# Feed-forward moved behind the attention, attention's lead loop and start reordered

## The reference

```python
y = gelu(x @ W.T + fc_bias + low_rank(x, side) + cond)
dots = q @ k.T * SCALE; pos_attn = q @ rel_emb[clip(i - j, -64, 64) + 64] * SCALE
x = x + softmax(dots + pos_attn) @ v @ Wo + bo
z = sigmoid(xz_t + h @ U_z + vz); r = sigmoid(xr_t + h @ U_r + vr)
hh = tanh(xh_t + r * h @ U + vh); h = (1 - z) * h + z * hh       # 256 steps, each needs the one before
sel = argmax(h @ gate_w.T); rw = sigmoid(max(h @ gate_w.T))
x = x + (u * silu(g)) @ w_down[sel], g = (rw * h) @ w_gate[sel].T, u = (rw * h) @ w_up[sel].T
```

## Time and profile before

| | before |
|---|---|
| runs, us | 614.16, 595.54, 595.69; median 595.69 |
| profiled execution, us | 597.63 |
| its span, first to last instruction, us | 595.5 |
| mean granted TensorE clock | 0.993 |
| TensorE busy | 571.2 us (96%) |
| VectorE busy | 403.6 us (68%) |
| ScalarE busy | 334.0 us (56%) |
| first and last write of hist | 84.2 and 585.3 us |

### The profile page before, as it was taken

How to read it: one execution, slowest core, us unless ns; L and a number is a source line. 1 busy time by engine, 2 the same in 40 slices (tenths; PEclk the granted TensorE clock), 3 DMA queues, 4 the chain that set the end, 5 groups by cost and what they waited for, 6 DMA issues and landing times.

```text
span 595.5 us, 16935 instructions
## 1 busy us (share of the span) xinstructions
PE 571.2 (96%) x5108; PEld 503.5 (85%) x5108; DVE 403.6 (68%) x2663; ACT 334.0 (56%) x1481; POOL 14.0 (2%) x41
## 2 busy tenths in 40 slices
PE   6999999999999999999999999999999999999996
PEld 5888778999989998899989998899889888776674
DVE  2447767777777777776777677777777777556654
ACT  2544436666666666666666666666666555323332
POOL 1140000000000000000000000000000000000000
PEclk9989999999999999999999999999999999999998
DMA  6155540222222212122212222222222210000000
GB/s 199 41 177 153 167 148 3 76 77 76 77 76 77 77 60 88 61 68 75 67 53 75 76 81 77 76 77 81 77 65 64 67 41 2 1 6 2 2 2 11
DMA packets 44194, 41.38 MB, mean 69 GB/s; under 512 B 5692, under 2 KB 43848, under 8 KB 43976
## 3 DMA queue, kind: packets, MB, share of 16 engines
q1 hardware_dynamic: 43520, 38.65, 21.8%
q10 hardware_dynamic: 584, 1.64, 0.8%
HBM read 20.95 MB, written 19.33 MB: 68 GB/s over the span
## 4 chain that ended last, share of the span: by engine, by line
PE 73%; DVE 11%; ACT 8%; issue 7%; DMA 1%; DVEq 0%; ACTq 0%
PE bank L359 66%; ACT p_sb L733 6%; PE bank L464 5%; DVE rinv L859 2%; ACT hh L806 1%; DVE pt_sb L867 1%; DVE g L998 1%; DVE sg L957 1%; DVE gm L943 1%; DMA x_nat<-in_x 1%; DVE sg L950 1%; PE bank L375 1%; PE bank L589 1%; DVE q L985 1%; DVE p_sb L861 0%
## 5 line engine op out<-in xcount | busy, mean ns | idle before, releaser
L359 PEld LDWEIGHTS bank<-q,uc 128*128 128x128 f32 x512 | 76.7, 189 | 28.0 <-DVE q L985 26.6
L806 ACT ACTIVATE hh<-bank 128x4 f32<-128x4 f32 x256 | 44.3, 173 | 95.2 <-PE bank L359 92.1
L359 PE MATMUL bank<-g,u 128*128 128x4 f32 x512 | 94.5, 255 | 3.1 <-DVE g L998 0.2
L359 PEld LDWEIGHTS bank<-b,uw 128*128 128x128 bf16 x1280 | 71.8, 97 | 28.6
L359 PE MATMUL bank<-hist,u 128*128 128x4 f32 x510 | 91.9, 251 | 0.3
L359 PE MATMUL bank<-q,uc 128*128 128x4 f32 x512 | 85.6, 238 | 6.6 <-DVE q L985 3.0
L359 PE MATMUL bank<-pt_sb,y_nat 128*128 128x128 f32 x512 | 88.9, 296 | 2.7 <-DVE pt_sb L867 2.3
L796 ACT ACTIVATE trz<-bank 128x4 f32<-128x4 f32 x256 | 44.3, 173 | 80.2 <-PE bank L359 78.2
L359 PE MATMUL bank<-yT,qp 128*128 128x256 f32 x256 | 85.4, 415 | 0.0
L359 PEld LDWEIGHTS bank<-g,u 128*128 128x128 f32 x512 | 76.8, 190 | 8.0 <-DVE g L998 7.8
L359 PEld LDWEIGHTS bank<-hist,u 128*128 128x128 f32 x510 | 77.4, 192 | 0.9 <-DVE hist L1002 0.2
(11 more groups left out here) (148 smaller groups left out, 956.8 us busy)
## 6 DMA issues: line engine op xcount, KB each, us to landing
skew<-e_sb SPq DMA_DIRECT2D x32, 574.0 KB, 3.4
pos<-skew SPq DMA_DIRECT2D x128, 128.0 KB, 2.6
wkv_sb<-in_L_attn_Wkv ACTq DMA_DIRECT2D x1, 1024.0 KB, 8.1
x_nat<-in_x SPq DMA_DIRECT2D x1, 512.0 KB, 4.8
wq_sb<-in_L_attn_Wq ACTq DMA_DIRECT2D x1, 512.0 KB, 6.0
wo_sb<-in_L_attn_Wo SPq DMA_DIRECT2D x1, 512.0 KB, 3.6
out<-y_out SPq DMA_DIRECT2D x8, 64.0 KB, 2.2
ffn_nat<-in_L_ffn_w_gate SPq DMA_DIRECT2D x1, 256.0 KB
```

The lines of the kernel that those rows point to most:

```text
L359: return pe.matmul(o, w_, x_, start=start, stop=stop, skip_group_check=True)
L806: act.activation(st["hh"][:, now, :], pre(2, c, k), ACT.Tanh).then_inc(hh_ok, 1)
```

## The change

- Feed-forward: tile 0 runs in steps 186 to 217, tiles 1 to 6 begin at steps 217, 222, ... 242 and take 16 steps each, so up to three overlap; tile 7 follows the loop as before. Tiles use banks 6/7, 2/3 and 4/5 in turn, and small tiles three buffers. In tiles 1 to 6 VectorE's half-tile products are whole-tile ones (512 columns). From step 217 on, the first piece of a step stands beside, further ones between. The copy of the result moves from VectorE to ScalarE.
- Fillers: as many as bring a step to two pieces between and two beside (one beside from step 217).
- Lead loop: move_pt(n - 1) behind sums(n), where move_pt(n - 2) stood ahead of it. SyncE writes quad q + 1 ahead of the reads of quad q, for q = 1 to 5.
- Start of step 0: the two zero products for banks 0 and 1 stand ahead of the last lead unit; the seeds are ScalarE's; two of three gate inputs stand behind the product of g in step 0.
- Head: even and odd heads' products alternate, jobs and banks are reordered, the first preps come earlier; the far columns of chunks 0 and 1 are left out, nothing reads them; TensorE multiplies zeros nine times before x arrives, and VectorE writes those zeros.

```diff
+JOBS = (("q", 0, 0), ("q", 1, 1), ("rel", 0, 2), ("k", 0, 3), ("k", 1, 0), ("A", 0, 1), ("A", 1, 2), ("R", 0, 7), ("R", 1, 6),
+        ("A", 2, 3), ("A", 3, 0), ("R", 2, 5), ("R", 3, 2), ("R", 4, 7), ("R", 5, 6),
+        ("v", 0, 3), ("v", 1, 0), ("y", 0, 5), ("y", 1, 2), ("B", 0, 7), ("B", 1, 6), ("B", 2, 3), ("B", 3, 0))
+SLOW_AT, FAST_AT, FAST_STEP = 186, 217, 5
+FAST_PE = {0: (0, 1), 1: (2, 3), 2: (4, 5), 3: (6, 7), 4: (8,), 10: (19,), 11: (21,), 12: (23, 24), 13: (25, 27), 14: (28,)}
+FAST_DVE = {1: (2,), 2: (4, 6), 3: (8,), 4: (11,), 6: (15,), 10: (17,)}
+FAST_ACT = {2: (6,), 4: (10,), 5: (14,), 11: (22,), 12: (26,), 15: (30,)}
+LAST_DVE = {1: (2,), 2: (4, 6), 3: (8,), 4: (10, 12), 6: (14, 16), 10: (18, 20)}
+FAST_LEN = 16
+AHEAD = 6
+F_BANKS = ((6, 7), (2, 3), (4, 5))
+GM_WHOLE, AH_WHOLE = range(1, TILES - 1), range(1, TILES - 1)
...
+        def tiles_at(t, of):
+            if SLOW_AT <= t < SLOW_AT + CT and not (of is FAST_DVE and t - SLOW_AT in (11, 15, 17)):
+                yield 0, t - SLOW_AT
+            for tau in range(1, TILES):
+                step = t - (T if tau == TILES - 1 else FAST_AT + FAST_STEP * (tau - 1))
+                for k in of.get(step, ()):
+                    yield tau, k
+
+        def upto(tau, half, whole):
+            before = sum(1 if i in whole else 2 for i in range(tau))
+            return before + (1 if tau in whole else half + 1)
+
+        def f_bank(tau, j):
+            return bank[F_BANKS[tau % 3][j]]
...
-                skew_quad(q)
+                if q < 2 or q > AHEAD:
+                    skew_quad(q)
+                if 1 <= q < AHEAD:
+                    skew_quad(q + 1)
                 for b in range(4):
                     unskew_unit(4 * q + b)
-                if q == 4:
+                if q == AHEAD:
...
+            def both_halves(j):
+                kind, a, _ = JOBS[j]
+                free(j)
+                free(j + 1)
+                heads = job_heads(kind, a)
+                for i, even in enumerate(heads):
+                    for e in range(2):
+                        h, o, half = even + e, bank[JOBS[j + e][2]], slice(e * DH, e * DH + DH)
                         if kind == "A":
                             ins = mm(o[:, i * D:(i + 1) * D], wqT[half, h // 2, :], wkT[half, h // 2, :])
                         elif kind == "R":
                             ins = mm(o[:, i * RELS:(i + 1) * RELS], wqT[half, h // 2, :], relT[half, :])
                         else:
                             ins = mm(o[:, i * D:(i + 1) * D], wvT[half, h // 2, :], wo_sb[half, h // 2, :])
-                ins.then_inc(job_pe, 1)
-
+                        if i == len(heads) - 1:
+                            ins.then_inc(job_pe, 1)
+
+            pe.wait_ge(zeros_ok, 1)
+            for k in range(9):
+                mm(bank[4][:, :], zeros[:, 0:128], zeros[:, :])
...
+                if n == LEAD - 1:
+                    pe.wait_ge(u_ok, 4)
+                    pe.wait_ge(pt_ok, LEAD - 2)
+                    pe.wait_ge(e_dve, PREP_LEAD // 4)
+                    pe.wait_ge(q_dve, PREP_LEAD // 4)
+                    for k in range(2):
+                        ins = mm(bank[k][:, :], uw[:, 0, :], zeros[:, :])
+                    ins.then_inc(bits_set, 1)
...
+            def filler(t=0):
+                tau, free = (t - FAST_AT) // FAST_STEP, bank[4]
+                if tau >= TILES - 1:
+                    pe.wait_ge(aT_ok, 2 * (TILES - 3))
+                    free = f_bank(TILES - 1, 0)
+                elif tau >= 1:
+                    pe.wait_ge(gm_ok, upto(tau, 1, GM_WHOLE))
+                    free = f_bank(tau, 0)
+                mm(free[:, 0:FILLER], uw[:, 0, :], zeros[:, 0:FILLER])
...
-            for gate in range(3):
-                gate_input(0, gate)
+            gate_input(0, 0)
...
             def between(t):
-                s = (t - 1) // 2
+                s, there = (t - 1) // 2, 0
                 if t % 2 == 1 and LEAD + s < UNITS:
                     scores(LEAD + s)
-                elif t % 2 == 1:
-                    filler()
-                elif t and PREP_LEAD + s < UNITS:
+                    there += 2
+                elif t and t % 2 == 0 and PREP_LEAD + s < UNITS:
                     prep(PREP_LEAD + s)
-                elif t:
-                    if s == UNITS - PREP_LEAD:
-                        pe.wait_ge(e_act, by_act(UNITS // 2 - 1))
-                        pe.wait_ge(q_act, by_act(UNITS // 2 - 1))
-                    filler()
-                    if LEAD + s - 2 < UNITS:
-                        filler()
+                    there += 2
+                if t % 2 == 0 and s == UNITS - PREP_LEAD:
+                    pe.wait_ge(e_act, by_act(UNITS // 2 - 1))
+                    pe.wait_ge(q_act, by_act(UNITS // 2 - 1))
+                if t > FAST_AT:
+                    for tau, k in list(tiles_at(t - 1, FAST_PE))[1:]:
+                        tile_stage(tau, k)
+                        there += 1
+                if t:
+                    for _ in range(2 - there):
...
+                s, there = t // 2, 0
+                if t % 2 == 0 and LEAD + s - 2 < UNITS:
+                    values(LEAD + s - 2)
+                    there += 2
+                if t % 2 == 1:
                     if LEAD + s - 1 < UNITS:
                         transposes(LEAD + s - 1)
+                        there += 1
                     if s == 0:
                         project(PROJ_LAG - 1)
                     if PROJ_LAG + s < UNITS:
                         project(PROJ_LAG + s)
-                    else:
-                        spare += 1
+                        there += 1
                 if t < CT:
                     weights(t)
-                else:
-                    tile_stage(t // CT - 1, k)
-                if PROJ_LAG + s >= UNITS - 4:
-                    for _ in range(spare):
-                        filler()
+                late = t >= FAST_AT
+                for tau, k in list(tiles_at(t, FAST_PE))[:1 if late else None]:
+                    tile_stage(tau, k)
+                    there += 1
+                for _ in range((1 if late else 2) - there):
+                    filler(t)
...
+                if t == 0:
+                    gate_input(c, 1)
+                if k == 0:
...
+            act.wait_ge(vb_ok, 1)
+            act.wait_ge(bits_set, 1)
+            for gate in range(3):
+                ins = seed(cp, 0, gate)
+            ins.then_inc(seed_ok, 1)
...
-                if n >= 2:
-                    move_pt(n - 2)
                 sums(n)
+                if n >= 1:
+                    move_pt(n - 1)
                 if n < PREP_LEAD - HEADS and n % 4 == 3:
                     move_eq((HEADS + n) // 2)
...
-            move_pt(LEAD - 2)
...
+                if k in (10, 11, 12):
+                    part = slice(0, 8) if k == 11 else slice(2 * k - 20, 2 * k - 16)
+                    n = part.stop - part.start
```

More of the change, by code:

```diff
@@ L323, in _ @@
                 pool.memset(iota[:, e:e + 1], float(e))
-            pool.memset(zeros[:, :], 0.0).then_inc(zeros_ok, 1)
             pool.wait_ge(setup_act, 6)
@@ L422, in _ @@
             pe.wait_ge(job_dve, 2)
-            for j in range(5, 19):
-                job(j)
-            pe.wait_ge(job_act, 8)
-            pe.wait_ge(job_dve, 7)
             def prep(m):
@@ L482, in project @@
                 mm(bank[5][:, 0:128], vo[:, h, :], z2[:, q % Z_RING, m % 4, :], start=(h == 0), stop=(h == HEADS - 1)).then_inc(pj_done, 1)
-            for m in range(4):
+            both_halves(5)
+            pe.wait_ge(setup_act, 4)
+            both_halves(7)
+            pe.wait_ge(job_act, 5)
+            pe.wait_ge(job_dve, 4)
+            for m in range(4):
+                prep(m)
+            both_halves(9)
+            both_halves(11)
+            both_halves(13)
+            job(15)
+            job(16)
+            for m in range(4, 6):
+                prep(m)
+            job(17)
+            job(18)
+            pe.wait_ge(job_act, 8)
+            pe.wait_ge(job_dve, 7)
+            for m in range(6, 8):
                 prep(m)
@@ L668, in _ @@
                 mm(pre(2, c, k), uc[:, :], st["q8"][:, now, :], start=False).then_inc(c_pre, 1)
-            for k in range(CT):
-                tile_stage(TILES - 1, k)
+            for tau, k in list(tiles_at(T - 1, FAST_PE))[1:]:
+                tile_stage(tau, k)
+            for t in range(T, T + FAST_LEN):
+                for tau, k in tiles_at(t, FAST_PE):
+                    tile_stage(tau, k)
         @block.scalar
@@ L698, in _ @@
                                bias=ybias[:, b:b + 1]).then_inc(setup_act, 1)
-            for j in range(4, 20, 2):
-                job(j)
             def move_e(duo):
@@ L818, in job @@
                 job_move(cp, kind, a, bank[at_bank]).then_inc(job_dve, 1)
+            dve.memset(zeros[:, :], 0.0).then_inc(zeros_ok, 1)
```

(2 more changed lines are left out.)

236 lines of the change are left out of this document (115 added, 121 removed).

## The result

| | before | after |
|---|---|---|
| runs, us (same chip) | 614.16, 595.54, 595.69, 625.02 | 618.01, 617.52, 618.38, 614.84 |
| median, us | 604.92 | 617.76 |
| profiled execution, us | 597.63 | 618.01 |
| its span, us | 595.5 | 616.2 |
| mean granted TensorE clock | 0.993 | 0.900 |

The change makes the kernel slower: the ratio is 1.036, 95% interval 1.033 to 1.039. The prediction was 566.8 us, within 559 to 577. One thing must be known to read the numbers: not every run of one kernel keeps the clock (of all 31 runs of the kernel before, ten took 612 to 630 us), and ratios leave such runs out. The changed kernel had lost it in all four.

A forecast was written before the change was run, and what follows sets the result against it. Bound: each step's serial loop through VectorE, TensorE and ScalarE, 1.78 us, plus some 0.2 of feed-forward above attention's 1.81. Terms -24.4 - 4.4 - 0.6 - 2.0 - 2.5 + 5.0 = -28.9 gave 566.8 us, range 559 to 577.

The forecast's parts named there:

- the term of the last 39 steps: Last 39 steps: overlapping feed-forward tiles lengthen steps through third pieces and whole-tile operations; +5.0 us on 70.3, bounds +1 and +12.
- Rival D: Attention's steps: with less work in each, the clock falls, 1.2 us more per step, kernel slower; 2%.
- Steps 32 to 185: Attention steps of the loop, freed of feed-forward: plain steps fall to 1.813 us; -24.4 us, bounds -18 and -26.
- Rival B: Attention's steps do not fall to 1.81 but stay at 1.90, 12 us come back, 579 us; 7%.
- The lead loop: 22 attention units ahead of step 0: pt copy behind the sums shortens gaps to 1.56 to 1.76; -4.4 us.
- From the last exp to step 0: Between lead loop and step 0: seeds on ScalarE, two gate inputs moved later; -0.6 us, bounds 0 and -1.5.
- The head: Start of the kernel: two terms, order of the jobs -2.0 us and products on zeros -2.5 us.
- The alternation: Head: neighbouring 64-row products on different row halves partly overlap; -2.0 us, bounds 0 and -3.5.
- The zeros: Head: nine products on zeros before x lands bring the full clock earlier; -2.5 us, bounds 0 and -4.
- SyncE: Lead loop: the quad written ahead covers the faster loop; a gap on pos would show SyncE too slow.
- A: Last 39 steps much dearer: three overlapping tiles hold the loop, 2.2 per step, 85.8 instead of 75.2, 577 us; 13%.
- both together: Dearer late steps and attention's steps not falling to 1.81 at once, about 590 us; 5%.

The follow-up runs named there:

- experiment 2: Changed kernel, counting only stages with TensorE work as pieces, and two things beside instead of one in the late steps; median 572.71 us, ratio 0.963.
- experiment 11: Changed kernel with two things beside from step 217 on, its piece count left as it is; median 573.55 us, ratio 0.963.
- experiment 3: Kernel before, with its fillers left out in steps 216 to 218 alone; median 632.16 us, ratio 1.063.
- Experiment 5: Kernel of experiment 2 with VectorE's e and q copies in two units and ScalarE's z copy ahead of its e copy; 570.15 us, one run.
- Experiment 6: Kernel of experiment 2 with VectorE's copy of pt ahead of the sums, as in the kernel before; 575.11 us, one run.
- experiment 9: Kernel of experiment 3 with 16 fillers in a row added in step 226; 607.89 and 610.64 us.
- experiment 8: Kernel of experiment 2 with all even heads' products, then all odd ones, instead of alternating; 573.95 us, one run.
- experiment 7: Kernel of experiment 2 with SyncE's order as before, no quad written ahead; 571.13 us, one run.
- experiment 4: Kernel of experiment 1 without the nine products on zeros ahead of x; 607.12 us, one run.
- experiment 10: Kernel of experiment 2 without the nine products on zeros ahead of x; median 572.64 us of four runs.
- experiment 12: Kernel of experiment 2 with the split copies of experiment 5, up to two pieces beside, fillers ahead of them; median 567.20 us, ratio 0.952.
- experiment 1: Changed kernel, counting only stages with TensorE work as pieces, still one thing beside in late steps; median 599.68 us of ten runs.

## Why the prediction was wrong, and where it was right

**The step that failed** is the term of the last 39 steps, "+5.0". Its durations were those of rows at the full clock, and its bounds, +1 and +12, held no case in which the clock changes. Rival D had the mechanism, but "in attention's steps", at 2%, with the seven plain steps at 1.00 as its counter-evidence. There the clock indeed held. The late steps of the change were not asked the same question, although the text on the order ahead of the prediction says of them: "Two fillers beside became one piece of the oldest tile, and one filler between became three pieces." The prediction costed fillers by their time alone, 0.03 per step, as if they had no other office. They are what holds the clock: 94 of them gave 70.3 us for these steps, 28 gave 119.8, 29 gave 101.7, 65 gave 75.5. Experiments 2 and 11 show this by the edit that undoes it, experiment 3 in the kernel before without the change. D's price per step was about right in form: 1.2 us more per step was put, and the 37 steps at half clock cost (119.8 - 75.5) / 37 = 1.2.

The trace of before held a sign of it, which neither the rows nor the prediction use. These windows of the kernel before (columns as above) lie on both sides of a fall at 37.64 us, ahead of the first exp:

```profile
34.20:37.60 3.40, 3.40 (x31) 3.40 (x30) 0.74 (x3) 1.33 (x4) 2.17 (x5) 1.00 0.81 248
37.60:41.00 3.40, 3.40 (x12) 2.91 (x12) 1.86 (x11) 1.94 (x5) 3.00 (x6) 0.51 0.15 43
```

TensorE was busy for all of the 3.40 us before, 22 of its 31 products having 16 or 4 columns, and the clock halved all the same. So a fall under a busy TensorE could be seen before the change ran, not only in the sparse tail that the prediction names.

**The same term with the clock held** was right: 75.5 in experiment 2 against 75.3 worked out. Its parts too: a full cycle of five steps took 1.82, 1.82, 2.05, 2.05 and 2.11, so that three pieces cost 0.23 (0.25 was put) and a whole-tile operation 0.3 in the step whose transposes wait for it. The prediction's 0.33 for these operations was spread over three of five steps, with q late in each; it came in one.

**Steps 32 to 185:** -24.4 was put, -23.5 came (285.1 us against 284.2). By kind the plain steps took 242.1 (241.1 was put), the closing ones 32.8 (32.8) and the opening ones 10.2 (10.3), so the working was right and not only its sum. Rival B is dead.

**The lead loop** was mis-sized: -4.4 was put, -0.9 came (39.45 against 40.38). Plain gaps are 1.57, as put; gaps with a prep and a projection are 1.57 as well, not the 1.76 that the prediction took for TensorE. What was missed are the copies. VectorE's e and q copies in four units were put at 0.3 each; they cost 0.8 to 1.1, and the units ahead of three of them 0.5 more (gaps of 2.05 to 2.09), which fits ScalarE's two prep copies ahead of the z copy there. Experiment 5 moves VectorE's and ScalarE's copies together and gets 36.4, near the 36.0 that the prediction had; the share of each was not measured apart. The last gap is another 0.76 above the plain ones: 2.33, where the kernel before had 1.90. There the two zero products for banks 0 and 1 wait for a copy of pt and stand ahead of the last unit's scores. The prediction had this wait, at about 0.4, but counted it behind the last exp. Experiment 6 shows that the pt copy was the link in the plain gaps. In the first 20 gaps the change gained 1.4 (38.48 to 37.12), and the last gave 0.4 back.

**From the last exp to step 0:** 5.0 became 4.05, -1.0 where -0.6 was put, in its bounds. With the 0.4 of the zero products, which fell into the lead loop, it is -0.5, near the -0.6 that was put.

**The head** gained 3.5 until the first exp (38.82 to 35.31) where 4.5 was put, but for another reason. In the profile before, the clock rose only at 17.2 us; in the same head of experiments 3 and 9 it rose at 8.7 and 8.9, and the first exp stood at 35.35 in experiment 3. So 3.5 us of the difference to the earlier trace rows is the luck of one execution before: the changed kernel gained nothing against that head (35.31), and 1.3 us where its clock held (34.02, experiment 2). The alternation is worth 2.2 (experiment 8) as put, -2.0, but the rest of the new order takes 0.9 of it back: without alternation it is 36.22 against 35.35 (one execution each; three executions of the new head with the clock full from 6 us on differ by up to 0.5: 33.63 in experiment 7, 34.11 in experiment 11). The zeros, put at -2.5, are worth 0 to 0.6 (experiments 4 and 10): the clock rises by 9 us without them. The clock could also fall again: in the changed kernel it was at half from 11.5 to 14.9 us, over the mix product (eight instructions 3.4 us; 1.9 in experiment 2), in experiment 2 not at all. This isn't due to the zeros alone, since in experiment 4, without them, it was at half from 12.4 to 15.8. The lower end of that term's bounds was the true one.

**SyncE:** no gap on positions was seen, and experiment 7 shows that the quad ahead is worth nothing at this pace. **Tail:** 0 put, 0.0 measured.

With the clock held the change gives 572.7 us, in the predicted range, 5.9 us above 566.8. About 3.7 of that are the terms (span 570.3 against 595.5 - 28.9 = 566.6): the lead loop's +3.5 and the attention steps' +0.9, with the head and the start of step 0 each 0.3 to 0.4 better. The other 2 come from the base: the terms were read from the profiled execution of 597.6 us, with its late clock, and taken off the median of 595.7.

One share in the prediction does not add up: by its own chances the range 559 to 577 leaves out half of A, B, D and both together, 20.5%, where it says about 18%. Nothing else hangs on it.

## What to carry to other kernels

- Products on zeros in a serial kernel are not slack to be filled with real pieces one for one. Before you replace them, list for each kind of step which products TensorE is given before and after, with their widths, instead of counting pieces, and look for the thinnest few steps.
- When a sum rests on durations at the full clock, give the case of the half clock its own price for each stretch of the program. Here it costs about 1.2 us per step and did not heal before the loop's end, so the price is that of all steps that follow.
- A loop that loses its critical link shows next the work that was hidden behind it. Read the units that carry extra copies, not the plain one.

## What the runs showed of the hardware that was not expected

- The clock fell with TensorE busy for 3.34 of 3.40 us, and stayed at 1.2 GHz for 119 us with TensorE busy throughout. The busy share of the profile is no guide to it. The Trainium skill (TensorE: Matmul & The Clock Gate, The HAM clock gate) says that activity releases the throttle; in those 119 us TensorE's activity, as the rows count it, did not.
- Holding and regaining differ. In the profiled run of the kernel before, steps with two to three fillers hold the full clock over the last 39 steps; after three steps without fillers the same steps stay at half for 112.6 us (experiment 3). There they mostly take 2.60 to 2.79 us each instead of 1.78, so the same fillers stand further apart; whether that is the reason no run separates. Sixteen fillers in a row bring it back within 5 us (experiment 9). That a few dense microseconds would be a cheap insurance in the changed kernel was not tried.
- The clock doesn't go by the number of fillers alone: 94, 65, 64 and 58 (experiment 12) in the last 39 steps held it in the profiled runs, 28 and 29 lost it, and so did the kernel before where seven were missing together, with 91 left in that stretch. Nor is the moment fixed by the program: experiments 1 and 4 have the same late steps, and the clock fell at 516.6 and at 507.4. Where between these the edge lies stays open. So does what it is in a filler that counts, its width, its type or the time that it fills, because no run put anything else in its place.
- The kernel before loses the clock in some of its runs with its fillers all there, and why stays open. As an estimate from the mean clock and span of eight such runs (0.918 of 627.6 us is 2 x 0.082 x 627.6 = 103 us at half, 0.953 of 611.8 is 58), they spend 57 to 103 us at half. None of them has a trace.
